# Products in array tiles moved behind the stages of a blockwise inverse, in a delta-rule attention kernel

## What is computed

```python
q = _short_conv(x @ Wq, conv_q)      # 4 taps and silu, also k and v, 3 each per token
q, k = _l2norm(q) * d ** (-0.5), _l2norm(k)
def step(S, inp):
    S = S * jnp.exp(gt)
    for i in range(3):
        kS = einsum('bhd,bhde->bhe', ki, S)
        S = S + bi * (ki[..., None] * (vi - kS)[:, :, None, :])
    o = einsum('bhd,bhde->bhe', qt, S)
o = o * rsqrt(mean(o * o) + 1e-05) * rms_weight * silu(x @ Wg)
x = _layernorm(x + o @ Wo)
x = _layernorm(x + ffn(x))           # top 2 of 8 experts
```

## Time and profile before

| | |
|---|---|
| three runs | 8206.38, 8210.04, 8248.30 us |
| median | 8210.04 us |
| the profiled execution | 8217.97 us |
| its span | 8215.9 us, mean granted TensorE clock 0.944 |
| PE busy (matmul) | 7423.3 us, 90% |
| DVE busy | 6459.2 us, 79% |
| ACT busy | 5469.5 us, 67% |
| POOL busy | 4117.8 us, 50% |

### The profile page before, as it was taken

The page is one execution under the profiler, slowest core; times in us unless marked ns, Lnnn a source line. Parts: engine busy times, 40 slices in busy tenths (PEclk is TensorE's granted clock), DMA queues, the critical chain, the costliest instruction groups (busy, mean ns, idle before and its releaser), DMA issues. The chain is left out here.

```text
span 8215.9 us, 426591 instructions
## 1 busy us (share of the span) xinstructions
PE 7423.3 (90%) x155940; PEld 6296.7 (77%) x155940; DVE 6459.2 (79%) x22300; ACT 5469.5 (67%) x20343; POOL 4117.8 (50%) x6333
## 2 busy tenths in 40 slices
PE   5889999999999999999999899999989999889999
PEld 3777777777787777777777777777777777757777
DVE  4888888888888888888888888888888888623333
ACT  3777777777777777777777777777777777533333
POOL 0555555555555555555555555555555555511111
PEclk6899999999999999999999999999999999889999
DMA  2000000000000000000000000000000000010000
GB/s 90 8 10 9 10 9 10 9 10 9 10 10 9 10 10 10 9 10 9 10 9 10 9 10 9 10 9 10 10 9 10 9 10 10 7 32 8 10 8 8
DMA packets 283626, 97.69 MB, mean 12 GB/s; under 512 B 226097, under 2 KB 276545, under 8 KB 281153
## 3 DMA queue, kind: packets, MB, share of 16 engines
q1 hardware_dynamic: 281408, 68.93, 3.8%
HBM read 52.08 MB, written 16.78 MB: 8 GB/s over the span
## 5 line engine op out<-in xcount | busy, mean ns | idle before, releaser
L819 DVE SCALAR_TENSOR_TENSOR CY<-PP,CWV,CY 128x128 f32<-128x128 f32 x4608 | 1585.5, 344 | 148.6 <-ACT CY L736 68.7
L819 DVE SCALAR_TENSOR_TENSOR CY<-PP,CWK,CY 128x128 f32<-128x128 f32 x4608 | 1581.4, 343 | 98.0 <-ACT CY L736 24.3
L1031 POOL TENSOR_TENSOR UM<-U,C 32x256 f32<-32x256 f32 x1536 | 1104.8, 719 | 120.2 <-POOL UM L1031 19.6
L1024 POOL TENSOR_TENSOR Y<-U,C 32x256 f32<-32x256 f32 x768 | 554.0, 721 | 1075.6 <-DVE UQ L912 1035.4
L550 PE MATMUL PI<-T,WB 32*32 32x32 f32 x49152 | 749.6, 196 | 303.2 <-DVE T L828 301.1
L550 PEld LDWEIGHTS PI<-T,WB 32*32 32x32 f32 x49152 | 639.0, 111 | 466.3 <-issue 403.2
L530 PE MATMUL PP<-XT,WV 128*128 128x131 f32 x3072 | 750.8, 328 | 188.5 <-issue 124.7
L530 PE MATMUL PP<-XT,WK 128*128 128x131 f32 x3072 | 783.6, 340 | 81.3 <-DVE CY L819 81.2
L736 ACT ACTIVATE CY<-PP,CWK 128x128 f32<-128x128 f32 x1536 | 564.4, 367 | 398.5 <-PE PP L530 387.4
L1004 POOL TENSOR_TENSOR S<-R,BETA 96x4 f32<-96x4 f32 x512 | 101.3, 198 | 1392.4 <-DVE R L872 1392.2
L736 ACT ACTIVATE CY<-PP,CWV 128x128 f32<-128x128 f32 x1536 | 567.2, 369 | 339.3 <-PE PP L530 328.0
(11 more groups left out here) (228 smaller groups left out, 18910.8 us busy)
## 6 DMA issues: line engine op xcount, KB each, us to landing
EX<-exd SPq DMA_DIRECT2D x768, 32.0 KB
exd<-EXS SPq DMA_DIRECT2D x16, 512.0 KB, 2.6
XR<-in_L_attn_x SPq DMA_DIRECT2D x65, 64.0 KB, 3.1
XL<-in_L_attn_x SPq DMA_DIRECT2D x16, 256.0 KB, 2.8
XRES<-in_L_attn_x SPq DMA_DIRECT2D x64, 64.0 KB, 2.7
x<-X SPq DMA_DIRECT2D x64, 64.0 KB, 3.1
XI<-x SPq DMA_DIRECT2D x16, 256.0 KB, 2.9
out<-OUT SPq DMA_DIRECT2D x16, 256.0 KB, 2.3
```

Of the source, the lines that this page charges most:

```text
L819: dve.scalar_tensor_tensor(CY[:, m % RING], ptile(m)[:, s:s + P], taps_of(m)[:, s:s + 1], CY[:, m % RING], ALU.mult, ALU.add).then_inc(tap ...
L1024: pool.tensor_tensor(Y1[r, :, :], U[r, par, :, r], over(first[r, :], [BK, NHEAD, BK], 1), ALU.mult).then_inc(seed_sb, 1)
L1031: pool.tensor_tensor(UM[r, lv], U[r, par, :, r], over(merge[lv][r, :], [BK, NHEAD, BK], 1), ALU.mult).then_inc(made, 1)
```

## The change

PE's slots are written in another order. Directly behind a stage of the inverse, ahead of the slot's projection, now stand the products that use array tiles: the second join (slot 4), the corner (slot 6), the gate (slots 8 and 10, c = 3), and the read-out, which moves from slot 11 to slot 12, as does ACT's copy of it. `rows_v` writes `PK` in slot 12 and `PA` in slot 13, and `old_state`, `rows_v` and DVE's `BZ` wait for the later count of `vp_sb` that this needs. The first join puts the products of even and odd heads at different partitions: `mid` at 32 to 63 and 0 to 31, `hi` at 64 to 95 and 96 to 127, so four column groups of the array are used instead of two, and ACT copies them in four instructions.

```diff
@@ views of PB
+        mids = PB[:, 0:4 * BK].rearrange("p (q c) -> p q c", q=4)
+        his = PB[:, 0:8 * BK].rearrange("p (q c) -> p q c", q=4)
@@ old_state, l == 0
-                        need(pe, vp_sb, min(2 * run + 3, 2 * NCH) if isinstance(run, int) else 2 * run + 3)
+                        need(pe, vp_sb, min(2 * run + 4, 2 * NCH) if isinstance(run, int) else 2 * run + 4)
@@ rows_v, l == 0
-                        need(pe, vp_sb, 2 * prep - 1)
+                        need(pe, vp_sb, 2 * prep)
@@ PE, in each slot: the blocks for the second join (k == 4), the corner (k == 6) and the gate
@@ (k in (8, 10)) now stand here, behind invert and ahead of project, unchanged, and then
+                        if k == 12 and do_run:
+                            read_out(run, rc)
                         if known(i, 0, NSC):
                             project(i, half, SLOTS * c + k)
...
                             for h in range(NHEAD):
-                                pe.matmul(join[mid, h, 0:BK], U[:, par, h, mid], X3[:, h, 0:BK], start=True, stop=True)
-                                mm = pe.matmul(join[hi, h], U[:, par, h, hi], X3[:, h], start=True, stop=True)
+                                q, o = h // 2, 1 - h % 2
+                                pe.matmul(mids[CT * o:CT * o + CT, q], U[:, par, h, mid], X3[:, h, 0:BK], start=True, stop=True)
+                                o = 2 + h % 2
+                                mm = pe.matmul(his[CT * o:CT * o + CT, q], U[:, par, h, hi], X3[:, h], start=True, stop=True)
...
-                        if k == 11 and do_run:
-                            read_out(run, rc)
...
                         if k in (12, 13) and do_prep:
-                            rows_v(k - 12, c, sc, prep, run, do_run)
+                            rows_v(13 - k, c, sc, prep, run, do_run)
@@ ACT
-                            act.activation(GA[BK:2 * BK, :, 0:BK], join[BK:2 * BK, :, 0:BK], ACT.Copy, scale=-1.0)
-                            act.activation(GA[2 * BK:R], join[2 * BK:R], ACT.Copy, scale=-1.0).then_inc(join_sb, 1)
+                            for e in range(2):
+                                o = CT * (1 - e)
+                                act.activation(GA[BK:2 * BK, e:NHEAD:2, 0:BK], mids[o:o + CT], ACT.Copy, scale=-1.0)
+                                o = CT * (2 + e)
+                                op = act.activation(GA[2 * BK:R, e:NHEAD:2], his[o:o + CT], ACT.Copy, scale=-1.0)
+                            op.then_inc(join_sb, 1)
...
-                        if k == 11 and do_run:
+                        if k == 12 and do_run:
                             act.wait_ge(o_ps, run + 1)
...
-                            l = k - 12
-                            act.wait_ge(vr_ps, 2 * prep + l + 1)
+                            l = 13 - k
+                            act.wait_ge(vr_ps, 2 * prep + k - 11)
@@ DVE, BZ
-                            dve.wait_ge(vp_sb, 2 * run + l + 1)
+                            dve.wait_ge(vp_sb, 2 * run + 2)
```

More of the change, by code:

```diff
@@ L640, in program @@
                             invert(invn, 1 - par, INV_AT[k])
[L641 to L651, removed]
-                                pe.matmul(join[mid, h, 0:BK], U[:, par, h, mid], X3[:, h, 0:BK], start=True, stop=True)
-                                mm = pe.matmul(join[hi, h], U[:, par, h, hi], X3[:, h], start=True, stop=True)
-                            mm.then_inc(join_ps, 1)
                         if k == 4 and do_run:
@@ L668, in program @@
                             mm.then_inc(join_ps, 1)
[L669 to L672, removed]
-                        if k == 11 and do_run:
-                            read_out(run, rc)
-                        if k in (10, 11) and do_run:
-                            new_state(k - 10, run, rc, prep, do_prep)
-                        if k in (12, 13) and do_prep:
-                            rows_v(k - 12, c, sc, prep, run, do_run)
[L679 to L690, removed]
                         if k in (8, 10) and gate_now:
@@ L705, in program @@
                             mm.then_inc(gate_ps, 1)
+                        if k == 12 and do_run:
+                            read_out(run, rc)
+                        if known(i, 0, NSC):
+                            project(i, half, SLOTS * c + k)
+                        if k in (1, 4) and do_run:
+                            old_state(k // 4, run, rs, rc)
+                        if k in (1, 3) and do_prep:
+                            rows_k(k // 2, i, c, sc, prep, run)
+                        if k == 2 and do_run:
+                            pe.wait_ge(x3t_sb, run + 1)
+                            side_bank_free(i, c, run, do_run)
+                            mid, hi = slice(BK, 2 * BK), slice(2 * BK, R)
+                            for h in range(NHEAD):
+                                q, o = h // 2, 1 - h % 2
+                                pe.matmul(mids[CT * o:CT * o + CT, q], U[:, par, h, mid], X3[:, h, 0:BK], start=True, stop=True)
+                                o = 2 + h % 2
+                                mm = pe.matmul(his[CT * o:CT * o + CT, q], U[:, par, h, hi], X3[:, h], start=True, stop=True)
+                            mm.then_inc(join_ps, 1)
@@ new lines, in program @@
+                        if k in (7, 9) and do_prep:
+                            gram(k // 9, c, sc, prep)
+                        if k in (8, 9) and do_run:
+                            solve(k - 8, run, prep, do_prep)
+                        if k in (10, 11) and do_run:
+                            new_state(k - 10, run, rc, prep, do_prep)
+                        if k in (12, 13) and do_prep:
+                            rows_v(13 - k, c, sc, prep, run, do_run)
+                        if k in (8, 10) and out_now:
+                            l = (k - 8) // 2
+                            if l == 0:
+                                need(pe, join_sb, 3 * run + 3 if do_run else 0)
+                                if not do_run:
+                                    side_bank_free(i, c, run, do_run)
+                            else:
+                                pe.wait_ge(ogt_sb, 2 * (i - 2) + 1)
+                            pe.wait_ge(og_sb, 2 * (i - 2) + l + 1)
+                            for h in range(LH):
+                                mm = pe.transpose(quad[:, h], OG[:, 2 * l + h // 2, h % 2], ident)
+                            mm.then_inc(ogt_ps, 1)
```

## The result

Slower: a median of 8520.4 us against 8208.2, a ratio of 1.042 (95% interval 1.038 to 1.045). The profiled execution took 8490.3 us, its mean granted TensorE clock is 0.884 in place of 0.944.

The account below looks back on a forecast made before the run. PE (slots 4 to 12) and DVE (slots 12 to 4) take turns. PE's part gets 1.39 us shorter; limited by DVE, 0.80 per step remains, times 255 = 204 us, giving 8006 us, range 7920 to 8180.

Parts of the forecast that it names:

- (e): First join, slot 2: four column groups instead of two save about 0.45 us of PE; worth on the path nought.
- the rival: TensorE's granted clock falls after the lengthened wait before stage 2, 3.4 us per fall; slower, to 8440 us; chance 0.17.
- (a): Second join moved directly behind stage 2 (slot 4): gain 0.28 us per step.
- (d): ACT gets the second join sooner, no longer stands 1.4 us in slot 4, freeing KD: gain 0.25 us.
- (b): Corner product moved directly behind stage 3 (slot 6), sparing the projection two edges: gain 0.19 us.
- (c): Read-out moved from slot 11 to behind stage 6, slot 12: stage 6 comes 0.67 us sooner, stage 7 loses 0.57 again.

Follow-up runs that it names:

- a2_join4: The kernel before with the first join in four column groups alone, and its four copies on ACT: 8675.5 us, 1.056.
- b3_no_join4: The changed kernel with the first join as before (two column groups, two copies): 8229.0 us, 1.003.
- c1_warm_full: The kernel before with slot 3's full-array projection issued again, 3 times more in c = 1 and 3, 9 in c = 2: 8087.9 us, 0.984.
- b2_copies4: The kernel before with PE's first join untouched (two column groups) and ACT's two copies of it cut into four: 8250.7 us, 1.0045.
- b1_join4_twice: The kernel before with the first join in four column groups, its products issued twice over, ACT's four copies kept: 8265.8 us, 1.006.

## Why the prediction was wrong, step by step

**The clock.** The step that failed is (e) at nought: the prediction knew that it lengthens PE's wait by 0.4 us and gave that no price in the sum. The runs show 467 us lost by (e) alone (a2_join4), and 291 us of the changed kernel's 312 come with it (8520.4 against 8229.0 in b3_no_join4). What kept it at nought is a sentence in the rival: "Against: 1.4 us is still far from 2.3." I took the two waits that I had looked at, 1.01 us with no fall and 2.3 us with one, as ends of a scale, and gave a wait in the middle a chance of 0.17. Mechanism, place and sign were those of the rival ("the wait that grows is the one before which the clock fell"); what I had against it was no evidence, and b3_no_join4 has the clock fall behind 1.17 us. My rows had the clock of four steps only; that it falls behind the turn of the loop too (above) I hadn't seen. And I let the rival end at 8440 us, two kinds of step in four. In the trace after, steps of all four kinds fall (clock 0.90, 0.83, 0.81 and, in the last 8 us, 0.52). The price of a fall, 3.4 us, is about that of the gate's step and the one behind it (30.76 for 27.50 us, 26.99 for 23.45), and twice that of the output step from which I had it: in c1_warm_full that step with the clock at 1.00 is shorter by 1.69 us (29.39 to 27.70). The time at the lower level can be worked out from the means: a mean of 0.884 between 0.5 and 1 is 23% of 8488 us, 1970 us; before, 0.944 is 920 us. From b2_copies4 (clock 0.937, 1040 us) to a2_join4 (0.879, 2100 us) the time rises by 425 us, 0.40 us for each us at the lower level.

**(e), the first join.** Its size on PE was right:

```profile
5103.62 0.22 PE L686 MATMUL PB<-X,U 96*32 96x32 f32 x1
...
5104.20 0.70 PE L552 MATMUL PI<-Y,WB 32*32 32x32 f32 x48
```

0.58 us from 1.02, 0.44 saved for the 0.45 estimated. I wrote "Its worth on the path is nought", because PE waits right behind it. At the full clock that holds: from stage 7 to the next stage 2, the stretch with the first join in it, the step takes 8.57 us after (5098.79 to 5107.36, below) and 8.55 before (5011.44 to 5019.99). But what PE saves there becomes wait, and the clock made of it the 467 us of a2_join4, of which b1_join4_twice gives 410 back. ACT's copies, two each:

```profile
L761 ACT ACTIVATE GA<-PB 32x256 f32<-32x256 f32 x14 | 5.3, 377 | 0.2
...
L759 ACT ACTIVATE GA<-PB 32x128 f32<-32x128 f32 x14 | 3.8, 268 | 0.2
```

2 x 377 + 2 x 268 = 1290 ns, for the 1270 estimated. I held them for hidden; b2_copies4 shows 41 us, between nought and the 79 that the prediction gives for them uncovered. The Trainium skill's rule on copies out of PSUM ("TensorEngine Tiling (Array Packing)", Performance Considerations) pointed the right way, though the 41 us are an eighth of the loss, and at a held clock, in the whole change, they don't show at all (8054.4 us with the four copies, 8064.2 without).

**(a) to (d), the order.** The step at the full clock, first PE's timeline after, from stage 2 to the next step's stage 2, then, from the kernel before, stages 6 and 7 ahead of the step of the earlier trace rows and that step's own stage 6:

```profile
5083.90 0.70 PE L552 MATMUL PI<-T,WB 32*32 32x32 f32 x48
5084.50 0.66 PE L648 MATMUL PB<-Y,GA 32*32 32x32 f32 x16
5085.09 0.49 PE L532 MATMUL PP<-XT,WV 128*128 128x131 f32 x2
...
5086.63 0.70 PE L552 MATMUL PI<-T,WB 32*32 32x32 f32 x48
...
5087.62 0.49 PE L532 MATMUL PP<-XT,WV 128*128 128x131 f32 x2
5088.39 0.49 PE L532 MATMUL PP<-XT,WV 128*128 128x131 f32 x2 [0.28 <-DVE CY L827]
5088.71 1.04 PE L581 MATMUL PK<-KQ 128*96 128x128 f32 x8
...
5096.73 0.70 PE L552 MATMUL PI<-T,WB 32*32 32x32 f32 x48
5097.36 0.65 PE L599 MATMUL PA<-BZ,UQ 128*32 128x128 f32 x16
...
5098.79 0.70 PE L552 MATMUL PI<-T,WB 32*32 32x32 f32 x48
...
5107.36 0.70 PE L552 MATMUL PI<-T,WB 32*32 32x32 f32 x48 [1.60 <-DVE T L836]
```

```profile
5009.95 0.70 PE L550 MATMUL PI<-T,WB 32*32 32x32 f32 x48
...
5011.44 0.70 PE L550 MATMUL PI<-T,WB 32*32 32x32 f32 x48
...
5033.83 0.70 PE L550 MATMUL PI<-T,WB 32*32 32x32 f32 x48
```

(a) From stage 2 to stage 3 it is 2.73 us (5083.90 to 5086.63), before 2.99: 0.26 for 0.28. (b) and (d): from stage 3 to `gram` 2.08 us (to 5088.71), before 2.00: 0.44 was expected, and nothing came. The two projections now stand together, and the second waits for DVE's taps, 0.28 us in brackets and 0.77 between starts. The wait of PE for ACT's KD became one for DVE. From there to stage 6 it is 8.02 us, before 8.85: 0.83, in which (c) is 0.67. In all 12.83 us from stage 2 to stage 6 in place of 13.84, a gain of 1.01 for the 1.39 of the sum. (c) then gives 0.57 of it back behind stage 6: from there to the next stage 2 it is 10.63 us (5096.73 to 5107.36), before 10.04 (5009.95 to 5019.99 in the earlier trace rows). I had expected that DVE hides part of this; DVE's row for stage 7 shows that it doesn't:

```profile
5099.74 0.42 DVE L836 TENSOR_TENSOR Y<-Y,PI 96x256 f32<-96x256 f32 x1 [0.33 <-PE PI L552]
```

It now waits 0.33 us there, in place of the 0.40 us for stage 6, which is gone. So the undisturbed step gains 0.42 us, not 0.75. Over all kinds of step the orders are worth 65 us at a held clock (8087.9 to 8023.3), for the 204 of the sum; without the hold they come out at nothing (8229.0 us). The output and gate steps, which I gave 0.85 us each, get nothing and 0.25.

**What was right:** that PE's slots 4 to 12 and DVE's 12 to 4 take turns, the 0.10 us for each edge of an array tile, that 32x32 followed by 128x32 costs as much as 32x32 followed by the full array (0.63 us from stage 3 to the corner), and three of the signs, PE's wait of over 350 us (387.5), the first join under 0.65 us (0.58) and ACT's wait ahead of L758's copy nearly gone (2.4). Three signs of being right didn't come: DVE is 92% busy in the undisturbed step (21.46 of 23.45 us) for over 96%, the step is 23.45 us for 23.1, and the projections behind the corner product are at 0.77 and 0.32 us for 0.34 and 0.22.

## What to carry to other kernels

Work in front of a wait on TensorE isn't free to remove: ask what the granted clock did behind the longest waits, and treat a wait that grows toward those as a likely loss, not as an unlikely one. A single wait's length is no safe sign: here the clock fell behind 1.17 us and stayed up behind 2.30. Where waits can't be removed, repeat a product in them that is already there, with few instructions for its time and no new semaphore, no more often than the wait takes (the larger number seems to have cost 41 us here), and measure each kernel under the same hold: compare held with held, not held with bare. That also goes for each change of order, since otherwise the clock's answer hides that of the order. And where two engines take turns, moving work from one's part to the other's is counted twice: once where it leaves, once where it lands.

## What the runs showed of the hardware that I had not expected

The clock fell behind one wait of 1.60 us and not behind another of 1.60 us in the same run, 112 us apart, and in b3_no_join4 behind 1.17 us and not behind 2.30; what else of the stretch decides is open. Added products held it whatever tile they used: 0.971 with 128x128, 0.971 with 128x32, 0.963 to 0.969 with 32x32, against 0.944 without. Two gains of 0.9% and 0.8% in the order of instructions came out together as a loss of 0.3%, with a clock of 0.944 and 0.950 alone and 0.923 together, though PE's wait ahead of stage 2 had not grown beyond that of one alone; at a held clock the two together are a gain of 65 us. And with 240 small products more in a loop body PE's idle time with no releaser doubled (132 to 260 us).
